# 4,096-key attention: one pair of maxima behind each group's masks, on quarters of the array, and the row sums beside the scores

## The reference

```python
x = x + _L0_xattn_ref(_layernorm(x), ctx_1024, ctx_1024)
x = x + _L0_attn_ref(_layernorm(x), ...)
x = x + _L0_ffn_ref(_layernorm(x), ...)
x = x + _L1_xattn_ref(ctx_1024, ctx_1024, _layernorm(x), mask_1x1xSxS2_ik0, w_out, b_out)
x = x + _L1_attn_ref(_layernorm(x), ...)
x = x + _L1_ffn_ref(_layernorm(x), ...)
```

```python
v = values.reshape(N, -1, HEADS, HEAD_DIM)
k = keys.reshape(N, -1, HEADS, HEAD_DIM)
q = queries.reshape(N, -1, HEADS, HEAD_DIM)
energy = jnp.einsum('nqhd,nkhd->nhqk', q, k)
energy = jnp.where(mask == 0, jnp.float32(-1e+20), energy)
attn = jax.nn.softmax(energy / math.sqrt(EMBED), axis=3)
out = jnp.einsum('nhql,nlhd->nqhd', attn, v).reshape(N, q_len, HEADS * HEAD_DIM)
return out @ w_out.T + b_out
```

## Time and profile before

| | us |
|---|---|
| median of 3 runs | 994.5 |
| lowest and highest | 984.84, 998.21 |
| the profiled execution | 993.12 |
| its span | 991.4 |

### The profile page before, as it was taken

The page is one execution under the profiler, slowest core; times in us unless marked ns, Lnnn a source line. Parts: engine busy times, 40 slices in busy tenths (PEclk is TensorE's granted clock), DMA queues, the critical chain, the costliest instruction groups (busy, mean ns, idle before and its releaser), DMA issues.

```text
span 991.4 us, 20180 instructions
## 1 busy us (share of the span) xinstructions
PE 945.7 (95%) x7230; PEld 556.7 (56%) x7230; DVE 595.1 (60%) x1543; ACT 455.2 (46%) x848; POOL 99.5 (10%) x135
## 2 busy tenths in 40 slices
PE   5999999999899999889999999999999999977998
PEld 5888885565466666644444444444444444456656
DVE  2455354653222212777777777777777777658883
ACT  3444434531021122566666666666666666642102
POOL 1223330002401011100000000000000000001000
PEclk9999999999899999999999999999999999999999
DMA  7744699116104733794554455544555444710000
GB/s 260 259 164 162 233 345 362 67 46 235 38 27 74 107 117 96 174 279 65 80 78 70 63 68 79 76 64 63 73 79 76 62 58 100 129 44 1 1 1 22
DMA packets 77731, 108.94 MB, mean 110 GB/s; under 512 B 27593, under 2 KB 63789, under 8 KB 73648
## 3 DMA queue, kind: packets, MB, share of 16 engines
q1 hardware_dynamic: 72376, 92.45, 42.8%
q0 software_dynamic: 5104, 15.36, 4.2%
q10 hardware_dynamic: 200, 0.44, 0.2%
HBM read 84.61 MB, written 21.82 MB: 107 GB/s over the span
## 4 chain that ended last, share of the span: by engine, by line
PE 83%; DVE 7%; DMA 3%; SPq 3%; issue 2%; ACT 1%; another core or an unknown queue 0%; POOL 0%; ACTq 0%; DVEq 0%
PE bank L1415 14%; PE bank L1436 13%; PE bank L1424 9%; PE bank L1282 8%; PE bank L1393 7%; PE bank L1085 5%; PE bank L1306 4%; PE bank L1072 4%; PE bank L1643 2%; PE bank L1447 2%; PE bank L1255 2%; PE bank L1167 1%; PE bank L1705 1%; PE bank L1176 1%; SPq L468 1%
## 5 line engine op out<-in xcount | busy, mean ns | idle before, releaser
L934 ACT ACTIVATE region<-bank 128x512 f32<-128x512 f32 x512 | 277.9, 595 | 156.5 <-PE bank L1424 156.5
L2076 DVE CUSTOM_DVE_ANT_0 xnT<-bank,region 128x1024 bf16<-128x1024 f32 x128 | 156.1, 1219 | 84.5 <-issue 84.5
L1415 PE MATMUL bank<-region 128*128 (+1 forms) x1024 | 157.1, 275 | 2.3 <-ACT region L934 1.8
L2076 DVE CUSTOM_DVE_ANT_0 region<-bank,region 128x1024 bf16<-128x1024 f32 x128 | 156.3, 1221 | 0.9 <-issue 0.5
L1436 PE MATMUL bank<-region 128*32 128x256 f32 x2048 | 138.9, 385 | 0.0
L1415 PEld LDWEIGHTS bank<-region 128*128 128x128 bf16 x1024 | 69.2, 97 | 119.5 <-issue 59.8
L1424 PE MATMUL bank<-region,identb 64*64 64x512 bf16 x1024 | 105.0, 400 | 0.0
L1436 PEld LDWEIGHTS bank<-region 128*32 128x32 f32 x2048 | 58.8, 109 | 34.3 <-ACT region L934 14.5
L1393 PE MATMUL bank<-region,xnT 64*128 64x512 bf16 x248 | 74.9, 382 | 1.6 <-DVE region L2076 1.1
L1282 PE MATMUL bank<-region 128*128 x240 | 75.2, 467 | 1.2 <-DVE region L1989 1.2
L1395 PE MATMUL bank<-region,xnT 64*128 64x512 bf16 x248 | 74.9, 382 | 0.0
(11 more groups left out here) (349 smaller groups left out, 1169.5 us busy)
## 6 DMA issues: line engine op xcount, KB each, us to landing
region<-keys_split SPq DMA_DIRECT2D x224, 128.0 KB, 5.0
region<-in_ctx SPq DMA_DIRECT2D x32, 512.0 KB, 6.4
keys_split<-region POOLq DMA_DIRECT2D x48, 256.0 KB, 4.3
region<-in_L_ffn_we_gate SPq DMA_DIRECT2D x8, 688.0 KB, 9.3
region<-in_L_ffn_we_up SPq DMA_DIRECT2D x8, 688.0 KB, 10.6
region<-in_L_ffn_we_down SPq DMA_DIRECT2D x8, 640.0 KB, 9.9
region<-in_mask_1x1xSxS_ik SPq DMA_DIRECT2D x1, 4096.0 KB, 17.0
mask_kept<-region SPq DMA_DIRECT2D x1, 2048.0 KB, 10.4
```

Of the source, the lines that this page charges most:

```text
L934: nc.scalar.activation(prob4[n % PROBS].rearrange("p a b -> p (a b)"), bank[:, SCORE4[n], :], ACT.Exp, scale=SCALE4).then_inc(exp4_ready, 1)
L1415: mm(bank[:, SCORE4[n], k * S:(k + 1) * S], slab[s][:, t * P:(t + 1) * P], qT4[:, bass.ds(u, 1), :].rearrange("p o q -> p (o q)"), start=( ...
L2076: v.tensor_tensor_reduce(out=junk[q], in0=bank[:, 3 + 2 * q:5 + 2 * q, :].rearrange("p a b -> p (a b)"), in1=maskN[:, q, 2 * c * CH:2 * (c ...
```

## The change

Five things, in the attention of the fourth block only:

- `max_pair` no longer waits; the wait is a function of its own, `max_banks_free`, and stands in the middle of a score group, between its two halves. The wait for the slab of the unit after the next moves there too.
- A pair of maxima is computed in four 64x64 products (two halves of the rows times two halves of the queries) instead of two 64x128 products. The same two banks get the same numbers. It counts up `max_psum` once instead of twice, and VectorE's wait counts so.
- One pair stands behind the masks of each group, instead of two behind each even group's masks.
- The row sums stand between the second score half and the masks of group 3, instead of behind the masks of group 3.
- Ahead of unit 0 the spin comes once ahead of each of the two pairs of unit 1, behind the wait for the slab and for the banks, instead of once ahead of that wait.

```diff
-            def max_pair(s, u, m):
-
-                q, c = m % 2, 2 * (m // 2)
-                b = 3 + 2 * (m % 2)
+            def max_banks_free(u, m):
+
                 k = u * MAXES + m
                 if not isinstance(k, int) or k >= 2:
                     pe.wait_ge(max_taken, k - 1)
+
+            def max_pair(s, u, m):
+
+                q, c = m % 2, 2 * (m // 2)
+                b = 3 + 2 * (m % 2)
                 if isinstance(u, int) and u == 0:
...
                 else:
-                    mm(bank[:, b, :], qmax4[s][0:64, q * P:(q + 1) * P], slab[s][0:64, c * CH:(c + 1) * CH], start=True, stop=True)\
-                        .then_inc(max_psum, 1)
-                    mm(bank[:, b + 1, :], qmax4[s][64:P, q * P:(q + 1) * P], slab[s][64:P, (c + 1) * CH:(c + 2) * CH],
-                       start=True, stop=True).then_inc(max_psum, 1)
+                    for h in range(2):
+                        for r in range(2):
+                            i, o = slice(64 * r, 64 * r + 64), 64 * (r ^ h)
+                            last = mm(bank[o:o + 64, b + r, :], qmax4[s][i, q * P + o:q * P + o + 64],
+                                      slab[s][i, (c + r) * CH:(c + r + 1) * CH],
+                                      start=True, stop=True, skip_group_check=True)
+                    last.then_inc(max_psum, 1)
...
-                def maxima(m):
-                    if m < MAXES:
-                        if left >= 1:
-                            max_pair(s1, u + 1, m)
-                    elif left >= 2:
-                        max_pair(s2, u + 2, m - MAXES)
-
                 def score_group(g):
-                    for n in (2 * g, 2 * g + 1):
-                        score_half(s, u, n)
+
+                    m = AHEAD + g
+                    s_m, u_m, n_m = (s1, u + 1, m) if m < MAXES else (s2, u + 2, m - MAXES)
+                    wanted = left >= (1 if m < MAXES else 2)
+                    score_half(s, u, 2 * g)
+                    if wanted:
+                        if m == MAXES:
+                            slab_there(s2)
+                        max_banks_free(u_m, n_m)
+                    score_half(s, u, 2 * g + 1)
+                    if g == 3 and not first:
+                        sum_rows(s - 1, u - 1)
                     score_mask(g)
+                    if wanted:
+                        max_pair(s_m, u_m, n_m)
 
                 pe.wait_ge(negT_ready, u + 1)
                 for j in range(PAIRS):
                     score_group(2 * j)
-                    if left >= 2 and AHEAD + 2 * j == MAXES:
-                        slab_there(s2)
-                    maxima(AHEAD + 2 * j)
-                    maxima(AHEAD + 2 * j + 1)
                     if between is not None:
                         between(j, False)
                     score_group(2 * j + 1)
                     if j == PAIRS - 1 and left >= 1:
                         negmax_T(u + 1)
-                    if j == 1 and not first:
-                        sum_rows(s - 1, u - 1)
...
             for m in range(MAXES):
                 pe.wait_ge(qT_ready, min(m + 1, QT))
+                max_banks_free(0, m)
                 max_pair(0, 0, m)
...
-            spin(2, 4)
             pe.wait_ge(slab_loaded[1], 16 * SLAB_LOADS)
             for m in range(AHEAD):
+                max_banks_free(1, m)
+                spin(2, 4)
                 max_pair(1, 1, m)
...
-                dve.wait_ge(max_psum, 2 * k + 2 - MAXES if not isinstance(k, int) or k >= MAXES else k + 1)
+                dve.wait_ge(max_psum, k + 1)
```

More of the change, by code:

```diff
@@ L1378, in queries_T @@
                 last.then_inc(qT_psum, 1)
+            def max_banks_free(u, m):
+                k = u * MAXES + m
+                if not isinstance(k, int) or k >= 2:
+                    pe.wait_ge(max_taken, k - 1)
             def max_pair(s, u, m):
@@ L1383, in max_pair @@
                 b = 3 + 2 * (m % 2)
-                k = u * MAXES + m
-                if not isinstance(k, int) or k >= 2:
-                    pe.wait_ge(max_taken, k - 1)
                 if isinstance(u, int) and u == 0:
```

## The result

The changed kernel takes 1015.6 us (median of 4 runs, 1012.0 to 1021.5) where the kernel before takes 996.4 (4 runs, 984.8 to 998.8): ratio 1.025, 95% interval 1.0195 to 1.0305. (The ratio is that of the fast runs and not the quotient of the two medians, which is 1.019.) It is slower: the whole interval lies above 1. The profiled execution took 1021.5 us with a span of 1019.8.

What follows compares the result with a forecast made beforehand. PE is busy throughout, but in even steps an equally long bank wait on ACT's exponential rules; odd steps are all PE. 993.1 + 26.8 - 3.7 + 1.4 = 1017.6, taken as 1017 us, range 1008 to 1028.

Steps and rivals of the forecast that it cites:

- the likeliest case: Whole kernel: slower, 1017 us, because pairs behind odd groups are exposed while even groups gain nothing; chance 0.79.
- The bank wait: Even group's masks to next odd group's: third score matmul waits for the even group's exponential; stays 1.42 us, gain nothing.
- One stream of 0.22 us in 122 odd steps: Odd group's masks to next even group's: the added maxima pair is exposed, 122 x 0.22 = +26.8 us.
- Quarters cost nothing and stream on behind the masks: Maxima pairs: four 64x64 matmuls run side by side, following the masks without a pause; cost nothing, bounds 0 to 0.22 per pair.
- Rival A: Behind odd groups: loads wait or only two quarters run together, so a pair costs 0.34, not 0.22; 1032 us, chance 0.12.
- VectorE's wait doesn't bite: Wait for maxima banks between score halves: costs nothing; bounds 0 to 0.3 us in one group of each unit.
- Row sums, -3.7: Group 3, sums behind same-form score matmuls: net -0.12 us in each of 31 units, up to -0.2 if the first load hides.
- Start, +1.4 (0 to 1.8): Start of the stage: two spins after the slab wait delay the maxima row's transpose by 1.8 and group 1's masks by 1.4 us.
- Rival B: Even to odd step: PE's own work sets 1.42, the bank wait has slack; -0.10 x 122, 979 us, chance 0.05.
- Rival C: Behind odd groups: the extra pairs are hidden by something not seen in the starts; 991 us, chance 0.04.

Runs made afterwards that it cites:

- e1_extra_even: The changed kernel with the maxima pair behind every even group computed twice; 1018.2 us in one run, first to last masks 467.8 us in both.
- e3_short_exp: The changed kernel with exponentials of halves 0 and 4 of units 1 to 31 over 256 of 512 columns; 1008.9 us in one run.
- e4_halves: The changed kernel with each maxima pair as two 64x128 products again, one pair behind each group; 1035.1 us, ratio 1.035 to the kernel before.
- e2_extra_odd: The changed kernel with the maxima pair behind every odd group computed twice; 1037.2 us in one run.
- e5_sums_back: The changed kernel with the row sums behind the masks and maxima pair of group 3 again, ahead of the values; 1029.4 us in one run.

## Why the prediction came out as it did

It said 1017 us, slower, by the likeliest case; 1015.6 was measured, and +24.5 us against the profiled execution stand beside +19.3 between the medians, whose own scatter is some us. The sum is better held against the trace, which gives the stage and its start: +20.9 from first masks to last, and 3.4 more from the slab wait to the first masks, 24.3 in all. By its steps:

- *The bank wait ends the even step at 1.42 us whatever PE does.* Right, shown from both ends (`e1_extra_even`, `e3_short_exp`). The loop's units kept 1.42 to 0.01 us. In 28 steps of the written-out units the wait ended 0.075 later, because of the second semaphore; 27 of them add 2.0 us, and one is part of the start below. That term was missing: the prediction weighed when VectorE would free the banks, and not in what form the PE waits for it.
- *One stream of 0.22 us in 122 odd steps, +26.8.* Right: 2.10 against 1.88, 26.3 us, and the doubling priced the same pair at 26.3 again. Inside the step the shares differ from my picture by 0.02 and 0.03: masks to maxima 0.24, maxima to values 0.31.
- *Quarters cost nothing and stream on behind the masks.* Right; as halves the odd step is 0.10 longer. Rival A falls: the loads run beside the masks on the same quarters (634.12 against 634.09).
- *VectorE's wait doesn't bite.* Right in mid-stage: from 500 to 880 us no matmul and no load waits for L2083. (Three loads, 1.2 us in all, are put down to VectorE's copy of the maxima row; the steps there are as long as elsewhere.) At the start it does bite, see below.
- *Row sums, -3.7.* Mis-sized: -6.1 (31 x 0.20), my upper bound. The masks of group 3 are late by 0.35, not by 0.43 to 0.46. The tail of 0.19 behind the sums was right, but the four starts lie 0.25 apart from first to last and not 0.33 to 0.36, as the second comes 0.03 behind the first where alone it came 0.13 behind: the first load has run beside the fourth score matmul, the case that I had kept for the bound.
- *Start, +1.4 (0 to 1.8).* Mis-sized, and outside its bounds: +2.1 from the end of the slab wait to the masks of group 1 (6.7 against 4.6). A spin holds the maxima up by 1.09 (432.47 less 431.38) and not by 0.9, and between the pairs another change of array shape comes with it: the transpose stands 2.9 us behind the wait's end (434.24 less 431.38) where it stood 0.5 (429.44 less 428.90), 2.3 later and not 1.8. The path was another one too. The wait for the maxima banks now stands inside group 0, so VectorE's L2083 holds group 0's second score half (436.25) and with it its masks, which come 3.4 later. The masks of group 1 follow them by the exponential's wait, 1.50 with the second semaphore, where they came 2.8 behind (433.46) as the second pair waited for VectorE.
- *Rival B, one mode change fewer makes it faster (979).* Its price was right and its condition not met: `e4_halves` against the changed kernel shows the 0.10 us a step that the missing mode change saves. It falls only on the odd steps, where it reduces a loss. The Trainium skill's rule that a change of tiling mode drains the array (TensorEngine Tiling (Array Packing), Key Properties) agrees with this trace, 0.34 against 0.24; what it can't tell is whether the drained time was on the path.
- *Rival C, hidden by something behind the odd groups.* Falls with `e2_extra_odd`.

The mechanism was right, and its term, 26.3 us, makes the loss. That the sum came within 0.2 us of the 24.3 is luck: errors of +2.4 (sums), +0.5 (the stream), -2.0 (second semaphore) and -0.7 (start) nearly cancel. So is part of the closeness of 1017 to 1015.6: the forecast was counted from one execution of 993.1, and the four runs before have their median at 996.4.

## What to carry to other kernels

An engine that is busy for 100% need not be all that sets the time: where its work and a wait on another engine are equally long, less work changes nothing. Take the work away in thought, or find a place in the trace where it is missing, as the last unit was here, and see if the step shortens. Work is free only in front of such a wait; spreading it evenly moves half of it to where it costs its full length. If a wait has a gap in front of it, put into it what fits the shape of its neighbours (here 0.36 us of row sums for 0.04), and give the instruction at the end of the wait no second semaphore.

## What I had not expected of the hardware

- A second semaphore on a weight load, in code whose waits are on constants, cost 0.075 us at the end of the wait (1.50 against 1.42 in 28 steps; with the other wait one matmul earlier 26 of them are 1.42, and the other two fall into a stretch at the lower clock).
- The second of the four fp32 sum matmuls starts 0.03 us behind the first when scores of the same array shape run ahead (673.61 and 673.64 in the changed kernel, below), and 0.13 behind when the mode has just changed (and again in `e5_sums_back`).

```profile
673.61 0.52 PE L1453 MATMUL bank<-summer,region 128*128 128x17 f32 x4
...
673.64 0.49 PE L1453 MATMUL bank<-summer,region 128*128 128x17 f32 x3
...
674.06 0.41 PE L1430 MATMUL bank<-region,identb 64*64 64x512 bf16 x4
```
